# Gathers of a graph network's edge rows, signalled and waited for by quad instead of by tile

## The reference

```python
edge_index = jnp.stack([src, dst])
h = jnp.maximum(_layernorm(x), 0.0); x = x + GCN(h)    # 2 convolutions, 128 -> 256 -> 128
h = jnp.maximum(_layernorm(x), 0.0); x = x + SAGE(h)   # 2 convolutions
h = jnp.maximum(_layernorm(x), 0.0); x = x + L2(h)     # 3 layers with edge attributes
h = jnp.maximum(_layernorm(x), 0.0); x = x + GAT(h)    # 4 attention layers, 2 heads
# the core of a convolution: take each edge's source row, weigh it, add up by destination
msgs = norm[:, None] * xw[src]
out  = jax.ops.segment_sum(msgs, dst, num_segments=n)
# a layer of L2
ea  = jax.nn.relu(edge_attr @ edge_w1[l] + edge_b1[l]) @ edge_w2[l] + edge_b2[l]
msg = hx[row] * w[:, None] + ea
```

## Time and profile before

| | |
|---|---|
| time, median of 3 runs | 5211.01 us (5206.4 to 5215.85) |
| the profiled execution | 5226.53 us, span 5224.8 us |
| busy share of the span: PE, DVE, ACT, POOL | 75%, 67%, 53%, 65% |
| gathers of line 1093 on POOL | 1568 by idx_all and 588 by idx_l, 1543.8 + 603.8 us busy |
| first and last gather of C1 to LB begin at | 1206.2 us and 3205.6 us |

### The profile page before, as it was taken

One profiled execution on the slowest core, in us unless ns is written; L12 is line 12 of the kernel. 1 busy time (PEld: TensorE's weight loads), 2 busy tenths in 40 slices (PEclk: granted clock), 3 DMA queues, 4 the chain that ended last, 5 costly groups with the idle time before them and its releaser, 6 DMA issues. The chain is left out here.

```text
span 5224.8 us, 117088 instructions
## 1 busy us (share of the span) xinstructions
PE 3910.9 (75%) x27481; PEld 3315.7 (63%) x27481; DVE 3497.0 (67%) x12527; ACT 2786.6 (53%) x7212; POOL 3413.1 (65%) x3998
## 2 busy tenths in 40 slices
PE   2888888888977698779999888665864966640176
PEld 1666666666866576778888777565764865640165
DVE  5888888886668766876666799327635833865433
ACT  2777777773434333656666688323522632430186
POOL 2666666665767576767567474575676667567577
PEclk9999999998988899999999999897997999875599
DMA  2776666664568676874334465794795788489443
GB/s 68 197 211 213 212 212 213 210 207 128 151 173 229 185 206 189 242 209 118 107 105 117 116 175 155 220 284 116 185 285 162 165 258 261 113 255 392 145 140 108
DMA packets 1087203, 971.64 MB, mean 186 GB/s; under 512 B 113214, under 2 KB 845974, under 8 KB 1087036
## 3 DMA queue, kind: packets, MB, share of 16 engines
q1 hardware_dynamic: 992956, 805.13, 50.6%
q0 software_dynamic: 94080, 164.48, 13.0%
HBM read 488.42 MB, written 484.70 MB: 186 GB/s over the span
## 5 line engine op out<-in xcount | busy, mean ns | idle before, releaser
L1093 POOL DMA_INDIRECT G<-table,idx_all x1568 | 1543.8, 985 | 758.8 <-issue 496.7
L1093 POOL DMA_INDIRECT G<-table,idx_l x588 | 603.8, 1027 | 291.5 <-issue 178.4
L1765 PE MATMUL PS<-G,S 128*128 (+1 forms) x2352 | 405.9, 290 | 27.8 <-DMA G<-table,idx_all 16.0
L1765 PE MATMUL PS<-CR,LO 97*128 97x128 f32 x2352 | 335.7, 288 | 67.8 <-ACT CR L2168 66.7
L1765 PEld LDWEIGHTS PS<-G,S 128*128 128x128 f32 x2352 | 351.0, 203 | 47.0 <-issue 29.0
L1765 PEld LDWEIGHTS PS<-S,G 128*128 128x128 f32 x1960 | 253.7, 195 | 168.2 <-issue 150.7
L1765 PEld LDWEIGHTS PS<-CR,LO 97*128 97x128 f32 x2352 | 303.6, 202 | 80.5 <-ACT CR L2168 79.5
L2168 ACT ACTIVATE G<-G 128x128 f32<-128x128 f32 x784 | 322.1, 483 | 60.4 <-issue 55.5
L1765 PE MATMUL PS<-S,G 128*128 128x128 f32 x1960 | 284.8, 287 | 92.6 <-DMA G<-table,idx_all 42.3
L1765 PE MATMUL PS<-G,FS 128*65 (+1 forms) x1764 | 276.4, 291 | 91.9 <-DMA G<-table,idx_all 52.8
L1765 PE MATMUL PS<-WX,OT 128*128 128x130 f32 (+1 forms) x2168 | 304.8, 285 | 36.9 <-ACT OT L2168 35.8
(11 more groups left out here) (381 smaller groups left out, 11146.4 us busy)
## 6 DMA issues: line engine op xcount, KB each, us to landing
table<-G SPq DMA_DIRECT2D x392, 256.0 KB, 3.4
table<-RO SPq DMA_DIRECT2D x271, 260.0 KB, 3.5
table<-RO SPq DMA_DIRECT2D x245, 256.0 KB
XIN<-xrows SPq DMA_DIRECT2D x196, 256.0 KB
table<-OWN SPq DMA_DIRECT2D x147, 260.0 KB
OWN<-table SPq DMA_DIRECT2D x139, 256.0 KB, 3.6
F<-table SPq DMA_DIRECT2D x132, 256.0 KB, 3.5
S<-table SPq DMA_DIRECT2D x100, 260.0 KB
```

The costliest lines, as they stand in the source:

```text
L1093: g.indirect_dma_start(G[:, t, 0:w], None, TAB[s], bass.IndirectOffsetOnAxis(ap=idx[:, t:t + 1], axis=0)).then_inc(gat[t % 4].sem, 16)
L1765: return nc.tensor.matmul(o, l, r, start=start, stop=stop)
```

## The change

In the seven stages the gathers of a quad add to one semaphore, `quad_in[n % 2]`, by turns. POOL waits once per quad, before its first gather, until the quad before the last one has landed. Each consumer waits once per quad until all four tiles have landed: in C1 and S1 before the first of the eight matmuls, in C2 and S2 before the six matmuls against FS, in LA and LB before the first product. The `gat` semaphores stay for X and the attended stages, where nothing else changes.

```diff
-        gat = [steps(f"gat{j}", {k: ("rows",) for k in KINDS}, 16) for j in range(4)]
+        gat = [steps(f"gat{j}", {k: ("rows",) for k in ("X",) + ATTENDED}, 16) for j in range(4)]
...
+        quad_in = [sem(f"quad_in{b}") for b in (0, 1)]
+
+        def gathered(s, n, h):
+
+            stages = [k for k in KINDS[:s] if k not in ("X",) + ATTENDED]
+            return n * 32 + (64 - 32 * h + 64 * len(stages) * ((QUADS + 1 - h) // 2))
...
                 for t in reversed(range(T)):
-                    if kind not in ATTENDED:
-                        pool.wait_ge(gat[t % 4].sem, gat[t % 4].at(s, LAST - t // 4))
+                    n = LAST - t // 4
+                    if kind not in ATTENDED and t % 4 == 3 and (s > 1 or n > 1):
+                        pool.wait_ge(quad_in[n % 2], gathered(s, n, n % 2) - 64)
+                    landed = gat[t % 4].sem if kind in ATTENDED else quad_in[n % 2]
                     g.indirect_dma_start(G[:, t, 0:w], None, TAB[s],
                                          bass.IndirectOffsetOnAxis(ap=idx[:, t:t + 1], axis=0)
-                                         ).then_inc(gat[t % 4].sem, 16)
+                                         ).then_inc(landed, 16)
...
             def messages(s, n, h):
 
                 dve.wait_ge(pd_e.sem, pd_e.at(s, n, "em"))
+                dve.wait_ge(quad_in[h], gathered(s, n, h))
                 for j in (3, 2, 1, 0):
-                    dve.wait_ge(gat[j].sem, gat[j].at(s, n, "rows"))
...
                 def rows_of(i):
                     if kind in ("LA", "LB"):
                         pe.wait_ge(mprod.sem, mprod.at(s, n, f"t{i}"))
-                    elif kind not in ATTENDED:
-                        pe.wait_ge(gat[i].sem, gat[i].at(s, n, "rows"))
...
                 pe.wait_ge(sel.sem, sel.at(s, n, f"t{j}"))
+                if j == 3 and kind in ("C2", "S2"):
+                    pe.wait_ge(quad_in[h], gathered(s, n, h))
                 if j == 3:
                     for i in (3, 2, 1):
...
                 for j in (3, 2, 1, 0):
                     pe.wait_ge(sel.sem, sel.at(s, n, f"t{j}"))
-                    if KINDS[s] != "GA":
-                        pe.wait_ge(gat[j].sem, gat[j].at(s, n, "rows"))
+                    if KINDS[s] != "GA" and j == 3:
+                        pe.wait_ge(quad_in[h], gathered(s, n, h))
```

## The result

The changed kernel takes 5223.64 us (median; 5215.11 to 5233.94), the kernel before, on the same chip, 5212.69 us (5203.67 to 5223.02). The ratio is **1.0023, 95% interval 1.0015 to 1.0032**: about 12 us slower. The forecast was 3 us slower.

What follows compares the result with a forecast made beforehand. C2, LA and LB were taken as bound by their consumers, S1 and S2 as paced by gathers. Terms -3.0 + 1.2 + 0.6 + 1.2 + 0.8 + 2.4 = +3.2 us on 5211 gave 5214 us; range 5202 to 5231, 8 in 10.

Steps and rivals of the forecast that it cites:

- the likeliest case: Whole kernel: the summed terms, +3.2 us on the median of 5211, give 5214 us; chance 0.62.
- -4 to +9: Whole kernel: stated bounds in us of the first two cases, giving 5203 to 5224 with the scatter between runs.
- a deeper queue of gathers is harmless: POOL: up to eight gathers in flight instead of some four cost nothing, as GA without waits has the same issue gap.
- POOL's waits that go: -3.0: POOL in the seven stages: waiting for landings goes, at most 6.1 us; the middle of the bounds was taken.
- C1: +1.2: PE at C1's start: six more matmuls after tile 0 lands, at the low clock; +1.2 us stays, bounds 0 and 4.
- S1: +0.6: PE in S1: six more matmuls after the last landing, at the high clock; +0.6 us once, after the last quad.
- S2: +1.2: PE in S2: twelve more matmuls after tile 0 lands, hidden by nothing; +1.2 us after the last quad, bounds 0 and 2.3.
- C2: +0.8: PE in C2: twelve more matmuls, partly replacing the wait for ACT's copy; +0.8 us, bounds 0 and 2.3.
- LA and LB: +2.4: DVE in both LA and LB: three more messages after tile 0 lands, +0.8 us in each stage; bounds 0 and 2.4.
- Instructions that go: 0: PE and DVE: dropped waits and register operations save nothing, being read ahead; bound 6.4 us at LB's first statistics.
- The clock in S2: Slower rival: one long PE wait lowers S2's clock towards C2's 0.81, up to 15 us, 5229 in all; chance 0.14.
- What would show it: Checks: POOL's gaps stay 0.30 us, S2's PE waits once per quad, tails and stages move 2 us at most, C1 4.

Runs made afterwards that it cites:

- eight everywhere: Kernel before with eight semaphores in the seven stages, GA and GZ, up to eight gathers in flight: consumers by tile 0.9972 and 0.997, by quad 0.9976.
- four by place: A semaphore for each of the four tiles of a quad, as in the kernel before: 5212.69 us beside the kernel after.
- four in pairs: Kernel after with four semaphores, tiles 3 and 1 of alternate quads on one, 2 and 0 on another: 0.9994; in GA and GZ too: 0.9991.

## Why the prediction was right or wrong

**The direction and the size.** Slower, by 12 us where 3 were forecast: inside the range, but beyond the likeliest case's own sum. Its "-4 to +9" is not what its bounds add up to, which is -6.1 to +11.6 (0 + 4 + 0.6 + 2.3 + 2.3 + 2.4), so that 12 lies at their upper end. By the runs the 12 us are made of three terms: about -8 for POOL's side with eight semaphores (0.9984, from 3 to 14 us), about +4 for the consumers (0.0006, plus or minus some 7 us), and about +12 for the shared semaphores (0.0024). Together +8, where the two runs of the kernel after have 8 and 12. That the time fell into the range was luck in part: a cost that no term stood for was offset by a gain larger than forecast.

**The step that failed** is the sentence that a deeper queue of gathers is harmless because GA shows it, with no wait at all and "the same 0.31 us". Depth is harmless indeed: eight deep with a semaphore for each is faster than before. But I let GA stand for everything on POOL that changes, and gave the shared semaphores no term; what the runs showed in its place are eleven gaps of 1.85 to 3.62 us and a cost of about 12 us. Nor was GA's queue deep: when a gather starts there, some two of those before it have rows to move, not eight. And GA's row held the warning. 195 gaps of 0.305 us are 59.5 us, GA has 60.8; the 1.3 us are one gap of 1.42 and one of 0.53, which the mean of 196 rounds away. The kernel before has such gaps in all its stages without waits, up to 2.16 us, and smaller ones in four of the seven with waits (1.13 us at most), and single gathers on POOL's timeline would have shown them.

**POOL's waits that go: -3.0, bounds 0 and -6.1.** Mis-sized. With eight semaphores the gain is about 8 us (3 to 14), so the bound of -6.1 fits better than the middle that I took; some 2 us of the 8 are gaps of the kernel before that no landing ended and that go as well. S2 alone gives 8 us in the profile, by 4.5 of gaps and 5 of shorter gathers, for which I had no term. My reason for the middle (a landing was late, and an earlier issue doesn't make transfers shorter) didn't hold: with a limit of eight the landings were no longer waited for at all.

**C1: +1.2.** Wrong in the detail. Quad 0's matmuls ended 1.32 us later after its first gather, as worked out, but by quad 2 nothing of it was left (-0.01). What C1 lost, 2.2 us, came from the gap at gather 113 (2.4 beyond the ordinary), and that did stay to the last quad (+2.15). The sentence that PE in C1 has no room to make up a delay was right, for a delay I hadn't foreseen.

**S1: +0.6, S2: +1.2, C2: +0.8.** Read from the two kernels with eight semaphores, POOL by quad, that differ in the consumers: S1's time from its last gather to the next stage is 18.6 against 18.7 us, C2's 42.1 and 42.1, S2's 20.5 against 19.3. So S2's term came as worked out (in the kernel after the last matmuls end 5.19 us after the last gather instead of 4.01), S1's and C2's did not appear there. That nothing hides S2's was wrong for most quads: PE stood before the carry matmuls for ACT's copy in 37 of 49. S2 as a whole is 4.2 us longer in that pair, and 6.7 in the pair with eight everywhere, where PE lost some 3.5 us to a late landing at quad 5 and kept that distance; these are single executions, and the timed pair has 4 us in all, plus or minus some 7.

**LA and LB: +2.4.** In the first of these pairs +0.0, +1.7 and +0.9, 2.6 in all: right, as far as single executions tell.

**Instructions that go: 0.** Right as far as a row tells: the 6.4 us of LB's first statistics were the bound, and they are still 6.4.

**Rivals.** The clock in S2 stayed (0.96). The long wait that the rival feared didn't come at every quad: PE waited for gathers before 20 of the 49. The wait for ACT's copy, which the rival had in its sum, did come, but PE's work of a quad with it took 4.79 us (2215.26 to 2220.05), below the 5.30, as argued against it. The section of the Trainium skill that was weighed there ("TensorE: Matmul & The Clock Gate", section "HAM oscillation — how this bites in real kernels") has a loop in which a burst of matmuls "is shorter than the DMA-wait for the next rhs slice". S2's quad shown above waits 1.72 us ahead of 3.9 us of matmuls in one run, so that this trace is no test of it. Nor is C2, whose clock is 0.81: in its middle, before the change, PE's waits are for ACT's copy (40.8 us in 29) and DVE's S (5.6 in 15), none for a gather.

**What would show it.** POOL has no idle time ended by a gather (right), but not the same 0.30 us before each (wrong: eleven times up to 3.62). The times after the last gather kept within 2 us in C1, S1, S2 and the first LA, and shrank by 3 in C2, the second LA and LB. There the gaps made the last gather late, but DVE or PE set the pace, and the stage's end hardly moved. That is why 26 us of gaps cost only about 12. No stage differs by more than 5 us: the largest is S1 with 3.1. But S1 and S2 (-2.7) pass the 2 us that the prediction allowed. In S2 PE didn't wait once per quad (20 of 49); LA's and LB's four messages are never broken by a wait (right).

## What to carry to other kernels

Merging completion signals of DMAs looks free, as fewer waits and fewer instructions; here two semaphores for up to eight gathers in flight cost 12 us over eight, and eight in all stages, with up to eight in flight, gained 16 us (0.3%) over the kernel before with four. When a row is to serve as proof that something is harmless, compare its idle total with the count times the ordinary gap, not means rounded to two digits, and look at single instructions for the outliers. Split a change that does three things before summing it: here POOL's side was a gain with eight semaphores, the later consumers a loss of a few us, and the shared semaphore, the part with no term, decided.

## What the runs showed of the hardware

Indirect DMAs of 128 rows on POOL have a recurring idle gap, at steps of 112 gathers with two semaphores and of 110 or a multiple with four by place, of up to 3.6 us, for which the rows of these runs name no releaser. It depends on which semaphores the gathers add to: two by parity of the quad, 1.7 to 3.6 us, ending with less than one gather, mostly none, left with rows to move; four by place, up to 2.5, with waits or without; four in pairs, or eight, none over 0.62. A limit of four in flight, put on GA and GZ that had none, cost 32 us. In the seven stages a limit of eight with eight semaphores gained 8 us over four with four; what the depth alone gives there is not shown.
